# Two perceiver attention stages, walked four units at a time instead of two

## Chip, cores and metric

One core of one Trainium2 chip. The metric is the device time of one launch in microseconds (us): TensorE (PE) does the matrix products, VectorE (DVE), ScalarE (ACT) and GpSimd (POOL) the elementwise work, SyncE (SP) starts DMAs. Everything here is float32.

## The reference, cut to what matters

Four layers of attention and feed-forward run one after the other over `x` of 8 x 256 x 256. The change touches the attention of layers 1 and 2 alone, called perceiver 1 (`p1`) and perceiver 2 (`p2`). For each of 8 batches:

```python
# layer 1 (perceiver 1): 8 heads of 64, keys and values from context rows and latent rows
kv = jnp.concatenate([layer_norm(ctx), layer_norm(latents)], axis=1) @ Wkv
k, v = jnp.split(kv, 2, axis=-1)
q, k, v = map(to_heads, (latents @ Wq, k, v))
q = l2norm(q) * q_scale
k = l2norm(k) * k_scale
sim = jnp.where(full_mask, jnp.einsum('bhid,bhjd->bhij', q, k) * SCALE, max_neg)
out = jnp.einsum('bhij,bhjd->bhid', softmax(sim), v)
return layer_norm(out @ Wo)
# layer 2 (perceiver 2): the same shape without mask, l2norm and the last layer_norm
```

`x + out` then goes to the next layer, whose LayerNorm statistics are taken as the sums are written.

## The kernel before

Softmax work is cut into **units**: one head, 128 query rows, 512 keys. There are 8 batches x 8 heads x 2 halves of the rows, so 128 units per perceiver. Eight units make a **group** `g` (one batch, four heads), 16 groups in all. A unit goes through five steps:

- scores (`scores`, PE): one product with 64 contraction rows and 512 columns. Two units of a pair sit in the upper and the lower 64 rows of the array.
- maximum (`largest`, DVE): in p1 one custom operation that adds the mask, negates and takes the minimum (L1692); in p2 a reduction (L1696).
- exponential with its sum (ACT, L1567 in p1, L1570 in p2).
- reciprocal and scaling (DVE, L1671 and L1673).
- four 128x128 transposes (PE, L1486), emptied by ACT (L1581); after four units `values` (PE, L1512) multiplies by V.

Besides the units there are **pieces**. `make` produces what the next group needs: j = 0 and 1 two halves of K, j = 2 the queries, j = 3 and 4 two halves of V, each 4 matrix products (L1445, L1449). In p1 each of j = 0 to 2 is then normed: square on ACT (`sq`, L1542), sum per head on DVE (`ss`, L1632), reciprocal root on POOL (`rs`, L206 and L207), product on DVE (`nrm`, L1637), transposes on PE (L1460), and a copy on ACT (L1548). In p2 DVE copies the first three out at once (L1644, L1646). `out` is the product by Wo for a whole batch (L1429, every second group); in p1 it is followed by statistics (DVE), reciprocal root (POOL), norm (DVE, L1619), an affine step of four operations (POOL, L1715 and L1716) and the residual sum (DVE, L215 to L217), in p2 by the residual sum alone. `context` norms, transposes and stores the next context rows.

Each engine runs its own list in program order and waits on counters. The lists are made by hand: `agenda` maps a place in units (steps of 0.5) to pieces, and all engines walk i = 0, 2, 4, ... with two units each time. PE gives the scores of units i and i+1, then transposes units i-2 and i-1, and the values come two to four units later; so an exponential has a whole round of other work on PE in front of its transposes. PSUM: banks 0 and 1 hold scores, 2 and 3 transposes, 4 values, 5 to 7 pieces.

Of the kernel before, what the change touches and what calls it, by code (L numbers as in the profile page):

```python
# [6 lines left out]
ALU = mybir.AluOpType  # L7
# [1275 lines left out]
class Perceiver:  # L1283
# [5 lines left out]
    N = 128  # L1289

    def __init__(self, k, which, heir, affine_x, affine_z):
# [35 lines left out]
        vs = (0, 0.5)  # L1327
        if which == 1:
            kq, context, out = (0, 0.5, 1.5, 2.5, 3), (0.5, 2.5, 3), (0, 0.5, 1, 2.5, 6, 7)
            steps, order = ((0, (0, 0.5, 1.5, 3, 1.75)), (1, kq), (3, kq), (4, vs), (5, vs)), (1, 0, 2, 3, 4)  # L1330
        else:
            context, out = (0, 2.5, 3), (0, 0.5, 1)
            steps, order = ((0, vs), (1, vs), (3, vs), (4, vs), (5, vs)), range(5)
        self.agenda = {}
        for g in range(16):
            if g > 0 and g % 2 == 0:
                self.spread(8 * g + 6, out, "out", g // 2 - 1, 0)
            if g < 15:
                for j in order:
                    self.spread(8 * g + steps[j][0], steps[j][1], "make", g + 1, j)  # L1340
            if g == 0 or g % 2 == 1 and g < 13:
                self.spread(8 * g + 4, context, "context", 1 if g == 0 else g // 2 + 2, 0)
        self.early = [("context", 0, 0, s) for s in range(3)] + [("make", 0, j, s) for j, s in ((0, 0), (3, 0), (3, 1))]
        self.first = []
        for x in range(40):
            for j, (at, parts) in enumerate(steps):
                if x / 4 - at in parts and ("make", 0, j, parts.index(x / 4 - at)) not in self.early:
                    self.first.append(("make", 0, j, parts.index(x / 4 - at)))
        self.last = [("out", 7, 0, s) for s in range(len(out))]
        takes_m, takes_u, takes_n = [], [], []  # L1350
        for i in range(-1, 2 * self.N + 9):
            for kind, g, j, s in (self.early + self.first if i < 0 else self.pieces(i / 2) if i < 2 * self.N + 8 else self.last):
                key = (kind, g, j)
                if s == (1 if kind == "context" else 0):
                    takes_m.append(key)
                if which == 1 and kind == "make" and j < 3:
                    if s == 1:
                        takes_n.append(key)
                    if s == 3:
                        takes_u.append(key)  # L1360
        self.M = Turns((6, 7) if which == 1 else (5, 6, 7), takes_m)
        self.U, self.Z = Turns((5,), takes_u), Turns((0, 1, 2), takes_n)
        k.leave()

    def spread(self, at, parts, *what):
        for s, part in enumerate(parts):
            self.agenda.setdefault(at + part, []).append((*what, s))

    def pieces(self, at):
        return self.agenda.get(at, ())  # L1370
# [10 lines left out]
    def free_m(self, t, key):  # L1381
        was = self.M.before(key)
        if was is None:
            return
        kind, g, j = was
        if kind == "context":
            t.wait_ge(self.cxe, g + 1)
        elif kind == "out":
            t.wait_ge(self.opx if self.which == 2 else self.oy, g + 1)
        elif j >= 3:  # L1390
            t.wait_ge(self.val, 2 * g + j - 2)
        else:
            t.wait_ge(self.nrm if self.which == 1 else self.made, 3 * g + j + 1)

    def free_z(self, seat, key):

        was = self.Z.before(key)
        if was is None:
            return
        seat.wait_ge(self.zt, 3 * was[1] + was[2] + 1)  # L1400
# [10 lines left out]
    def pe_piece(self, t, kind, g, j, s):  # L1411
        k, key = self.k, (kind, g, j)
        if kind == "context":
            if s == 1:
                bk = k.bank(self.M.bank(key))
# [6 lines left out]
        elif kind == "out":  # L1422
            if s < 2:
                bk = k.bank(self.M.bank(key))
                if s == 0:
                    self.free_m(t, key)
                    t.wait_ge(self.oev, 2 * g + 2)
                for c in range(4):
                    ins = t.e.matmul(bk[:, s * 256:(s + 1) * 256], self.OT[:, c, s * 128:(s + 1) * 128], self.wo[:, c, :],  # L1429
                                     start=c == 0, stop=c == 3)  # L1430
                if s == 1:
                    ins.then_inc(self.opm.sem, 1)
        elif s == 0:
            b, hg = divmod(g, 2)
            at = slice(hg * 256, hg * 256 + 256)
            bk = k.bank(self.M.bank(key))
            self.free_m(t, key)
            t.wait_ge(*self.ready_w)
            half = (0, 1, 1, 0, 1)[j]
            x = self.rows_of(t, b, half)  # L1440
            w = (self.wk, self.wk, self.wq, self.wv, self.wv)[j]
            if j >= 3 or self.which == 1:
                for i in range(2):
                    for c in range(2):
                        ins = t.e.matmul(bk[:, i * 256:(i + 1) * 256], x[:, c, i * 128:(i + 1) * 128], w[:, c, at], start=c == 0, stop=c == 1)  # L1445
            else:
                for i in range(2):
                    for c in range(2):
                        ins = t.e.matmul(bk[:, i * 256:(i + 1) * 256], w[:, c, hg * 256 + i * 128:hg * 256 + (i + 1) * 128], x[:, c, :],  # L1449
                                         start=c == 0, stop=c == 1)  # L1450
            ins.then_inc(self.vmm.sem if j >= 3 else self.mm.sem, 1)
        elif s == 3:
            z, T, e = self.kn[self.Z.bank(key)], k.bank(5), 3 * g + j
            was = self.U.before(key)
            if was is not None:
                t.wait_ge(self.made, 3 * was[1] + was[2] + 1)
            t.wait_ge(self.nrm, e + 1)
            for c in range(2):
                for i in range(2):
                    ins = t.e.transpose(T[:, (2 * c + i) * 128:(2 * c + i + 1) * 128], z[:, i * 256 + c * 128:i * 256 + (c + 1) * 128], k.ident[:, :])  # L1460
            ins.then_inc(self.zt.sem, 1)

    def pe(self, t):
# [8 lines left out]
        for i in range(0, self.N + 4, 2):  # L1472
            if i < self.N:
                self.scores(t, i)
                self.scores(t, i + 1)
            for x in range(2):
                for at in (i + x, i + x + 0.5):
                    for p in self.pieces(at):
                        self.pe_piece(t, *p)
                u = i - 2 + x  # L1480
                if 0 <= u < self.N:
                    T = k.bank(2 + u % 2)
                    t.wait_ge(self.pt, u - 1)
                    t.wait_ge(self.scaled, u + 1)
                    for j in range(4):
                        ins = t.e.transpose(T[:, j * 128:(j + 1) * 128], self.P[u % 4][:, j * 128:(j + 1) * 128], k.ident[:, :])  # L1486
                    ins.then_inc(self.turned.sem, 1)
# [1195 lines left out]
```

## Time and profile before

| | |
|---|---|
| time, median of 3 runs | 1835.99 us (1834.31 to 1837.7) |
| profiled execution | 1833.89 us, of which the span 1832.1 us |
| busy share of the span | PE 86%, DVE 57%, ACT 49%, POOL 21% |
| chain that ended last | PE 69%, DVE 15%, ACT 6%, issue 5%, POOL 2% |

The share of an engine is the sum of its records over the whole span. The chain is followed back from the last instruction, at each step to what released it. p1's units run from about 519 to 908 us, p2's from about 1049 to 1405 us, about 40% of the span together.

### The profile page before, as it was taken

To read this page: it belongs to the slowest core of one execution; us is meant where nothing else is said; L and a number is where in the kernel's file an instruction comes from. 1 tells how busy PE (TensorE), PEld (TensorE's weight loads), DVE (VectorE), ACT (ScalarE), POOL (GpSimd) and SP (SyncE) were. 2 spreads that over 40 slices of the span, in tenths; PEclk is the share of its full clock that TensorE was granted. 3 is DMA by queue.
4 is the path that set the end of the run, shared out by engine and by line. 5 is a ranking of instruction groups with operands and counts; after the bars stand their busy time and mean duration, and the time that the engine had idled before them with its cause. 6 is when DMAs were issued, how large, how long until landed. Compare 5 with 4: busy or idle time off the path is not lost.

```text
span 1832.1 us, 27965 instructions
## 1 busy us (share of the span) xinstructions
PE 1579.8 (86%) x9902; PEld 1199.2 (65%) x9902; DVE 1050.6 (57%) x2956; ACT 906.7 (49%) x2034; POOL 380.5 (21%) x480
## 2 busy tenths in 40 slices
PE   7999958999489999999868799999998749995566
PEld 5677637999357676676536666666665548994444
DVE  7767752211546676766577665555555424325887
ACT  4888821332156666666449355555554102323366
POOL 1000014111232333323140100000001332323734
PEclk9999988999799999999978899999999979997889
DMA  9000027998300000000000200000000328993001
GB/s 339 6 1 1 2 92 305 323 330 290 118 7 7 7 7 7 7 1 1 1 1 1 81 12 7 6 7 6 1 1 12 138 81 297 355 348 112 1 12 35
DMA packets 61882, 154.08 MB, mean 84 GB/s; under 512 B 9232, under 2 KB 39696, under 8 KB 55248
## 3 DMA queue, kind: packets, MB, share of 16 engines
q1 hardware_dynamic: 54352, 135.73, 21.6%
q0 software_dynamic: 5280, 14.47, 2.1%
q10 hardware_dynamic: 2112, 2.10, 0.4%
q8 instruction: 80, 1.31, 0.3%
q14 instruction: 58, 0.48, 0.1%
HBM read 135.71 MB, written 24.75 MB: 88 GB/s over the span
## 4 chain that ended last, share of the span: by engine, by line
PE 69%; DVE 15%; ACT 6%; issue 5%; POOL 2%; DMA 1%; another core or an unknown queue 1%; POOLq 1%; SPq 0%; DVEq 0%; ACTq 0%
PE bank L1024 8%; PE bank L1445 8%; PE bank L974 7%; PE bank L1499 7%; PE bank L1512 6%; PE bank L1486 5%; PE bank L1449 5%; PE bank L1429 3%; PE bank L679 3%; PE bank L1851 2%; PE bank L695 2%; PE bank L710 1%; ACT p1f L1567 1%; PE bank L616 1%; POOL small L207 1%
## 5 line engine op out<-in xcount | busy, mean ns | idle before, releaser
L1696 DVE TENSOR_REDUCE small<-bank 128x1 f32<-128x512 f32 x128 | 82.4, 686 | 108.7 <-PE bank L1499 108.7
L1043 ACT ACTIVATE e2a<-bank,WB 128x128 f32<-128x128 f32 x156 | 44.6, 368 | 177.6 <-PE bank L1024 122.7
L1692 DVE CUSTOM_DVE_ANT_0 p1f<-bank,p1f 128x512 f32<-128x512 f32 x128 | 83.2, 687 | 81.3 <-PE bank L1499 81.3
L1570 ACT ACTIVATE p2f<-bank,small 128x512 f32<-128x512 f32 x128 | 86.9, 683 | 86.2 <-DVE small L1696 86.2
L751 ACT ACTIVATE l<-l,small 128x256 f32<-128x256 f32 x256 | 108.9, 502 | 32.6 <-DVE small L817 32.2
L1567 ACT ACTIVATE p1f<-p1f,small 128x512 f32<-128x512 f32 x128 | 91.2, 713 | 67.9 <-DVE small L1692 67.6
L400 POOL TENSOR_SCALAR rs<-mv 128x4 f32<-128x4 f32 x16 | 3.6, 228 | 566.7 <-DVEq L230 551.7
L817 DVE CUSTOM_DVE_ANT_0 l<-bank,small 128x256 f32<-128x256 f32 x256 | 90.8, 420 | 13.4 <-PE bank L695 12.5
L1445 PE MATMUL bank<-WA,HT 128*128 128x256 f32 x384 | 93.1, 386 | 5.0 <-DVE p1f L1637 5.0
L1581 ACT ACTIVATE p2f<-bank 128x512 f32<-128x512 f32 x128 | 75.2, 599 | 40.5 <-PE bank L1486 39.0
L1043 ACT ACTIVATE e0a<-bank,WB 128x128 f32<-128x128 f32 x128 | 36.6, 368 | 102.1 <-PE bank L1024 102.1
L207 POOL TENSOR_TENSOR small<-small,nhalf 128x8 f32<-128x8 f32 x48 | 80.5, 1678 | 4.0
L1581 ACT ACTIVATE p1f<-bank 128x512 f32<-128x512 f32 x128 | 74.2, 590 | 13.2 <-PE bank L1486 13.2
L1445 PEld LDWEIGHTS bank<-WA,HT 128*128 128x128 f32 x384 | 70.3, 193 | 14.6 <-DVE p1f L1637 5.6
L1024 PEld LDWEIGHTS bank<-e2a,WB 128*128 128x128 f32 x624 | 75.6, 192 | 5.8 <-issue 3.9
L1024 PE MATMUL bank<-e2a,WB 128*128 128x128 f32 x624 | 76.2, 274 | 3.1 <-DVE e2a L1192 3.1
L1486 PE MATMUL bank<-ident,p1f 128*128 128x128 f32 x512 | 75.0, 275 | 3.4 <-ACT p1f L1581 2.2
L1486 PEld LDWEIGHTS bank<-ident,p2f 128*128 128x128 f32 x512 | 61.0, 141 | 23.6 <-ACT p2f L1581 13.3
L1486 PEld LDWEIGHTS bank<-ident,p1f 128*128 128x128 f32 x512 | 59.9, 141 | 24.5 <-ACT p1f L1581 17.4
L1499 PE MATMUL bank<-p1f 64*128 64x512 f32 x256 | 73.5, 644 | 2.2 <-ACT p1f L1548 2.2
L1486 PE MATMUL bank<-ident,p2f 128*128 128x128 f32 x512 | 74.7, 275 | 0.0
L1499 PE MATMUL bank<-p2f 64*128 64x512 f32 x256 | 73.6, 641 | 1.1 <-ACT p2f L1570 1.1
(388 smaller groups left out, 3832.2 us busy)
## 6 DMA issues: line engine op xcount, KB each, us to landing
WB<-in_L2pack SPq DMA_DIRECT2D x39, 514.0 KB
WB<-in_L2pack SPq DMA_DIRECT2D x39, 512.0 KB
WB<-in_L0pack SPq DMA_DIRECT2D x16, 1028.0 KB
WB<-in_L0pack SPq DMA_DIRECT2D x16, 1024.0 KB
e0a<-in_L0pack SPq DMA_DIRECT2D x7, 1028.0 KB
e0a<-in_L0pack SPq DMA_DIRECT2D x7, 1024.0 KB
sorted_h<-in_blank SPq DMA_DIRECT2D x6, 1032.0 KB, 16.2
e2a<-sorted_h SPq DMA_DIRECT2D x39, 129.0 KB
```

The source lines that it names most:

```text
L207: g.e.tensor_tensor(dst, dst, self.nhalf[:, 0:n], ALU.pow).then_inc(flag.sem, 1)
L751: ins = a.e.activation(P[:, h * 256:(h + 1) * 256], P[:, h * 256:(h + 1) * 256], ACT.Exp, scale=-1.0, bias=self.mx[:, m + h:m + h + 1])
L817: ins = v.e.tensor_tensor_reduce(P[:, h * 256:(h + 1) * 256], k.bank(x)[:, h * 256:(h + 1) * 256], self.causal[:, h, :], -1.0, 3.0e38, ALU ...
L974: ins = t.e.matmul(y[:, 0:256], self.gb[i % 2][:, c, :], w[:, self.n1 + c * 256:self.n1 + (c + 1) * 256], start=c == 0, stop=c == nf - 1)
L1024: ins = t.e.matmul(bk[:, j * 128:(j + 1) * 128], w[:, c * ff + ft * 128:c * ff + ft * 128 + 128], self.xT[i % 2][:, c, :], start=c == 0, s ...
L1445: ins = t.e.matmul(bk[:, i * 256:(i + 1) * 256], x[:, c, i * 128:(i + 1) * 128], w[:, c, at], start=c == 0, stop=c == 1)
L1449: ins = t.e.matmul(bk[:, i * 256:(i + 1) * 256], w[:, c, hg * 256 + i * 128:hg * 256 + (i + 1) * 128], x[:, c, :], start=c == 0, stop=c == 1)
L1486: ins = t.e.transpose(T[:, j * 128:(j + 1) * 128], self.P[u % 4][:, j * 128:(j + 1) * 128], k.ident[:, :])
L1499: t.e.matmul(k.bank(i % 2), self.Q[g % 2][rows, c, a * 128:(a + 1) * 128], self.K[g % 2][rows, c, :], start=True, stop=True).then_inc(self ...
L1512: ins = t.e.matmul(k.bank(4)[64 * o:64 * o + 64, c * 256:c * 256 + 256], self.V[g % 2][:, j, h * 64:(h + 1) * 64], self.PT[n % 2][o][:, j, ...
L1567: ins = a.e.activation(P, P, ACT.Exp, scale=-1.0, bias=self.mx[:, m:m + 1], accum_out=self.sm[:, m:m + 1])
L1581: a.e.activation(self.PT[u // 4 % 2][o][:, :, h * 128:(h + 1) * 128], k.bank(2 + u % 2).rearrange("p (k n) -> p k n", k=4), ACT.Copy).then ...
```

## The change

The four steps of a walk (scores, maxima, exponentials, transposes) now take four units at a time, a **visit**; 32 visits per perceiver, `q` = 0 to 31. Group g has visit a = 2g and visit b = 2g+1. Inside a visit each engine has numbered parts, and the agenda is written with (engine, visit, part). Transposes of a visit's own units follow in the same visit, and `values` opens the next one. Scores and transposes of unit u share bank u mod 4, and banks 5 to 7 serve all pieces, p1's transposes of keys and queries included, which go back into the bank of their product. DVE takes the maxima of units 0 and 1 in part 0, of units 2 and 3 in part 1, and scales in parts 2 and 3; its pieces stand ahead of the unit work of their part. The sums and the number of operations are the same.

```diff
-        for i in range(0, self.N + 4, 2):
-            if i < self.N:
-                self.scores(t, i)
-                self.scores(t, i + 1)
-            for x in range(2):
-                for at in (i + x, i + x + 0.5):
-                    for p in self.pieces(at):
+        for q in range(self.QUADS + 1):
+            if q:
+                self.values(t, q - 1)
+            if q == self.QUADS:
+                break
+            for x in range(4):
+                self.scores(t, 4 * q + x)
+            for x in range(4):
+                if x % 2 == 0:
+                    for p in self.pieces("pe", q, x // 2):
                         self.pe_piece(t, *p)
...
+                self.turn_unit(t, 4 * q + x)
+            for p in self.pieces("pe", q, 2):
+                self.pe_piece(t, *p)
...
+                for j, at in ((0, (a, 0, a, 0)), (1, (a, 0, a, 0)), (2, (a, 1, a, 2)), (3, (b, 0, b, 0)), (4, (b, 0, b, 2))):
+                    if self.which == 1 and j == 3:
+                        put("pe", b, 0, "make", n, 1, "turn")
+                    put("pe", at[0], at[1], "make", n, j, "mm0")
+                    put("pe", at[2], at[3], "make", n, j, "mm1")
+                    if self.which == 1 and j == 2:
+                        put("pe", a, 2, "make", n, 0, "turn")
+                    if self.which == 1 and j == 4:
+                        put("pe", b, 1, "make", n, 2, "turn")
+                if self.which == 1:
+                    for j, sq, ss, rs, nrm, ev in ((0, (a, 1), (a, 3), (a, 2), (a, 4), (b, 0)), (1, (a, 2), (a, 4), (a, 3), (a, 5), (b, 1)),
+                                                   (2, (b, 0), (b, 1), (b, 0), (b, 3), (b, 3))):
+                        put("ac", *sq, "make", n, j, "sq")
+                        put("dv", *ss, "make", n, j, "ss")
+                        put("po", *rs, "make", n, j, "rs")
+                        put("dv", *nrm, "make", n, j, "nrm")
+                        put("ac", *ev, "make", n, j, "ev")
...
+                else:
+                    for j, ev in ((0, (a, 2)), (1, (a, 3)), (2, (b, 0))):
+                        put("dv", *ev, "make", n, j, "ev")
...
+                    put("dv", b + 1, 1, "out", o, 0, "st")
+                    put("po", b + 1, 0, "out", o, 0, "fac")
+                    put("dv", b + 1, 2, "out", o, 0, "nrm")
+                    put("po", b + 1, 1, "out", o, 0, "aff")
+                    put("dv", b + 2, 4, "out", o, 0, "add")
+                else:
+                    put("dv", b + 1, 1, "out", o, 0, "add")
...
+        for q in range(self.QUADS):
+            for pt in range(6):
+                for p in self.pieces("dv", q, pt):
                     self.dv_piece(v, *p)
+                if pt < 2:
+                    self.largest(v, 4 * q + 2 * pt)
+                    self.largest(v, 4 * q + 2 * pt + 1)
+                elif pt < 4:
+                    self.scale_unit(v, 4 * q + 2 * pt - 4)
+                    self.scale_unit(v, 4 * q + 2 * pt - 3)
```

ACT takes the four exponentials, with the pieces of part 1 in the middle, then empties the four transposes.

(In the new file, the scores are L1519, transposes L1527, values L1540, `make` L1479 and L1481, maxima L1735 and L1739, reciprocal L1719, scaling L1721, context transposes L1440, POOL's affine step L1758 and L1759.)

**PE in p2, four units.** Before, two pairs of scores (L1499) with `make` products and transposes (L1486) between, up to the values (L1512):

```order
L1499 MATMUL bank<-p2f 128x512 x2
L1449 MATMUL bank<-WB 128x256 x4
L1486 MATMUL bank<-ident,p2f 128x128 x4
L1449 MATMUL bank<-HT,WB 128x256 x4
L1486 MATMUL bank<-ident,p2f 128x128 x4
L1499 MATMUL bank<-p2f 128x512 x2
L1486 MATMUL bank<-ident,p2f 128x128 x4
L1449 MATMUL bank<-HT,WB 128x256 x4
L1486 MATMUL bank<-ident,p2f 128x128 x4
L1512 MATMUL bank<-p2f 64x256 x8
```

After, one visit b: behind the four scores stand the product j = 3 and the first half of j = 4, then all sixteen transposes of the visit, the second half of j = 4 and the context transposes (L1440):

```order
L1519 MATMUL bank<-p2f 128x512 x4
L1479 MATMUL bank<-WB 128x256 x4
L1479 MATMUL bank<-WB,HT 128x256 x2
L1527 MATMUL bank<-ident,p2f 128x128 x16
L1479 MATMUL bank<-WB,HT 128x256 x2
L1440 MATMUL bank<-ident,p2f 128x128 x4
L1540 MATMUL bank<-p2f 64x256 x8
```

The two islands of scores have become one, and the transposes now belong to the units whose scores stand just ahead.

**DVE in p2, where the residual sum of a finished batch stands.** Before, it followed the maxima and scalings of a pair:

```order
L1696 TENSOR_REDUCE small<-bank 128x1 x2
L1671 RECIPROCAL small<-small 128x1
L1673 TENSOR_SCALAR p2f<-p2f,small 128x512
L1671 RECIPROCAL small<-small 128x1
L1673 TENSOR_SCALAR p2f<-p2f,small 128x512
L215 TENSOR_TENSOR X<-bank,X 128x256
L200 BN_STATS st<-X 128x6
L201 BN_AGGR mv<-st 128x2
L217 TENSOR_TENSOR X<-bank,X 128x256
L200 BN_STATS st<-X 128x6
L201 BN_AGGR mv<-st 128x2
L1696 TENSOR_REDUCE small<-bank 128x1 x2
```

After:

```order
L1739 TENSOR_REDUCE small<-bank 128x1 x2
L215 TENSOR_TENSOR X<-bank,X 128x256
L200 BN_STATS st<-X 128x6
L201 BN_AGGR mv<-st 128x2
L217 TENSOR_TENSOR X<-bank,X 128x256
L200 BN_STATS st<-X 128x6
L201 BN_AGGR mv<-st 128x2
L1739 TENSOR_REDUCE small<-bank 128x1 x2
L1719 RECIPROCAL small<-small 128x1
L1721 TENSOR_SCALAR p2f<-p2f,small 128x512
```

The sum has moved between the second and the third maximum of a visit, ahead of the first scaling.

**POOL in p1, at the end of a batch.** Before, the reciprocal root of the output (rs) was followed by those of three `make` pieces (small), and the affine step came last:

```order
L207 TENSOR_TENSOR rs<-rs,nhalf 128x2
L206 TENSOR_SCALAR small<-small 128x8
L207 TENSOR_TENSOR small<-small,nhalf 128x8
L206 TENSOR_SCALAR small<-small 128x8
L207 TENSOR_TENSOR small<-small,nhalf 128x8
L206 TENSOR_SCALAR small<-small 128x8
L207 TENSOR_TENSOR small<-small,nhalf 128x8
L1715 TENSOR_TENSOR WB<-WB,rows 128x256
L1716 TENSOR_TENSOR WB<-WB,rows 128x256
L1715 TENSOR_TENSOR WB<-WB,rows 128x256
L1716 TENSOR_TENSOR WB<-WB,rows 128x256
```

After:

```order
L207 TENSOR_TENSOR rs<-rs,nhalf 128x2
L1758 TENSOR_TENSOR WB<-WB,rows 128x256
L1759 TENSOR_TENSOR WB<-WB,rows 128x256
L1758 TENSOR_TENSOR WB<-WB,rows 128x256
L1759 TENSOR_TENSOR WB<-WB,rows 128x256
L206 TENSOR_SCALAR small<-small 128x8
L207 TENSOR_TENSOR small<-small,nhalf 128x8
L206 TENSOR_SCALAR small<-small 128x8
L207 TENSOR_TENSOR small<-small,nhalf 128x8
L206 TENSOR_SCALAR small<-small 128x8
L207 TENSOR_TENSOR small<-small,nhalf 128x8
```

The four affine operations have moved ahead of the three reciprocal roots on which the next group's keys and queries wait.

## Rows read from the trace of the kernel before

**Rows 1.** Busy time by engine in stretches of p1 (two) and p2

```profile
core 0: us, PE busy (x) PEld busy (x) DVE busy (x) ACT busy (x) POOL busy (x), PEclk, DMA share, GB/s
518.70:534.00 15.30, 14.38 (x63) 9.82 (x64) 9.52 (x25) 8.65 (x18) 5.49 (x6) 0.89 0.01 1
534.00:907.60 373.60, 365.82 (x2134) 254.97 (x2134) 249.03 (x675) 235.46 (x517) 115.47 (x134) 1.00 0.02 5
1049.50:1405.00 355.50, 353.63 (x2021) 244.73 (x2020) 208.62 (x485) 194.27 (x445) 0.00 (x0) 1.00 0.02 5
```

**Rows 2.** Timeline of PE in p1: start us, us, engine, line, operation, count

```profile
601.48 0.60 PE L1486 MATMUL bank<-ident,p1f 128*128 128x128 f32 x4
602.01 1.95 PE L1512 MATMUL bank<-p1f 128*64 128x256 f32 x16
603.89 1.13 PE L1499 MATMUL bank<-p1f 64*128 64x512 f32 x4
604.95 1.99 PE L1445 MATMUL bank<-WA,WB 128*128 128x256 f32 x8
606.78 0.60 PE L1486 MATMUL bank<-ident,p1f 128*128 128x128 f32 x4
607.22 1.89 PE L1445 MATMUL bank<-WA,HT 128*128 128x256 f32 x8
608.95 0.60 PE L1460 MATMUL bank<-ident,p1f 128*128 128x128 f32 x4
```

**Rows 3.** Timeline of p2 near its end, scores to reciprocal

```profile
1393.95 1.13 PE L1499 MATMUL bank<-p2f 64*128 64x512 f32 x4
...
1395.11 1.29 DVE L1696 TENSOR_REDUCE small<-bank 128x1 f32<-128x512 f32 x2 [1.65 <-PE bank L1499]
1395.84 0.69 ACT L1570 ACTIVATE p2f<-bank,small 128x512 f32<-128x512 f32 x1 [1.17 <-DVE small L1696]
...
1396.65 0.16 DVE L1671 RECIPROCAL small<-small 128x1 f32<-128x1 f32 x1 [0.25 <-ACT p2f L1570]
```

**Rows 4.** Timeline of DVE in p1, scalings back to back

```profile
558.44 0.16 DVE L1671 RECIPROCAL small<-small 128x1 f32<-128x1 f32 x1
558.63 0.49 DVE L1673 TENSOR_SCALAR p1f<-p1f,small 128x512 f32<-128x512 f32 x1
559.03 0.16 DVE L1671 RECIPROCAL small<-small 128x1 f32<-128x1 f32 x1
```

**Rows 5.** Timeline near p1's end, POOL, scaling, its transposes

```profile
891.36 0.79 POOL L1716 TENSOR_TENSOR WB<-WB,rows 128x256 f32<-128x256 f32 x1
...
891.67 0.76 DVE L1673 TENSOR_SCALAR p1f<-p1f,small 128x512 f32<-128x512 f32 x1
...
892.55 0.42 PEld L1486 LDWEIGHTS bank<-ident,p1f 128*128 128x128 f32 x4 [0.45 <-issue]
```

**Rows 6.** Timeline of p1's drain, emptying and values

```profile
904.57 1.09 ACT L1581 ACTIVATE p1f<-bank 128x512 f32<-128x512 f32 x2 [0.26 <-PE bank L1486]
905.71 0.29 PEld L1512 LDWEIGHTS bank<-p1f 128*64 128x64 f32 x4 [0.93 <-ACT p1f L1581]
```

**Rows 7.** Timeline of a norm in p1, ss to nrm

```profile
510.21 0.69 DVE L1632 TENSOR_REDUCE small<-p1f 128x8 f32<-128x512 f32 x1 [4.21 <-ACT p1f L1542]
510.99 0.24 POOL L206 TENSOR_SCALAR small<-small 128x8 f32<-128x8 f32 x1 [5.71 <-DVE small L1632]
...
513.01 0.69 DVE L1637 TENSOR_TENSOR p1f<-bank,small 128x512 f32<-128x512 f32 x1 [2.12 <-POOL small L207]
```

**Rows 8.** Timeline of p1's last output, statistics to affine step

```profile
913.46 0.43 DVE L200 BATCH_NORM_STATS2 st<-bank 128x6 f32<-128x256 f32 x1 [9.40 <-PE bank L1429]
...
915.85 1.00 DVE L1619 TENSOR_SCALAR WB<-bank,mv,rs 128x256 f32<-128x256 f32 x2 [1.21 <-POOL rs L207]
916.92 0.72 POOL L1715 TENSOR_TENSOR WB<-WB,rows 128x256 f32<-128x256 f32 x1 [1.18 <-DVE WB L1619]
...
919.33 0.72 POOL L1716 TENSOR_TENSOR WB<-WB,rows 128x256 f32<-128x256 f32 x1
```

**Rows 9.** Timeline of p2's last residual sum, both halves

```profile
1409.53 0.42 DVE L215 TENSOR_TENSOR X<-bank,X 128x256 f32<-128x256 f32 x1 [8.73 <-PE bank L1429]
...
1410.55 0.39 DVE L217 TENSOR_TENSOR X<-bank,X 128x256 f32<-128x256 f32 x1
```

More of the change, by code:

```diff
@@ new lines, in __init__ @@
+        self.first = [("make", 0, j, p) for j, p in order]
+        self.last = [("out", 7, 0, p) for p in ("mm0", "mm1", "st", "fac", "nrm", "aff", "add")]
+        takes = [x[0:3] for x in self.early + self.first if x[3] in ("turn", "mm") and (x[0] == "context" or x[3] == "mm")]
+        for q in range(self.QUADS):
+            for pt in range(3):
+                takes += [x[0:3] for x in self.pieces("pe", q, pt) if x[3] == {"context": "turn", "make": "mm0", "out": "mm0"}[x[0]]]
+        self.M = Turns((5, 6, 7), takes + [("out", 7, 0)])
@@ L1334, in __init__, with plan @@
+        k.leave()
+    def plan(self):
         self.agenda = {}
+        put = self.put
         for g in range(16):
-            if g > 0 and g % 2 == 0:
[L1337 to L1340, printed above, removed]
-            if g == 0 or g % 2 == 1 and g < 13:
-                self.spread(8 * g + 4, context, "context", 1 if g == 0 else g // 2 + 2, 0)
@@ L1343, in __init__ @@
[L1343 to L1360, printed above, removed]
@@ L1372, in weights, with put, pieces @@
+            if g == 0 or g % 2 == 1 and g < 13:
+                c = 1 if g == 0 else g // 2 + 2
+                put("dv", b - 1, 5, "context", c, 0, "norm")
+                put("pe", b, 2, "context", c, 0, "turn")
+                put("ac", b + 1, 0, "context", c, 0, "ev")
+    def put(self, engine, q, pt, *what):
+        self.agenda.setdefault((engine, q, pt), []).append(what)
+    def pieces(self, engine, q, pt):
+        return self.agenda.get((engine, q, pt), ())
     def weights(self, W, ready):
@@ L1392, in free_m @@
         else:
[L1393 to L1400, printed above, removed]
+            t.wait_ge(self.made, 3 * g + j + 1)
     def rows_of(self, seat, b, j):
@@ L1428, in pe_piece @@
                 for c in range(4):
-                    ins = t.e.matmul(bk[:, s * 256:(s + 1) * 256], self.OT[:, c, s * 128:(s + 1) * 128], self.wo[:, c, :],
+                    ins = t.e.matmul(bk[:, i * 256:(i + 1) * 256], self.OT[:, c, i * 128:(i + 1) * 128], self.wo[:, c, :],
                                      start=c == 0, stop=c == 3)
-                if s == 1:
+                if i == 1:
                     ins.then_inc(self.opm.sem, 1)
[L1433 to L1456, printed above, removed]
+        elif s == "mm":
+            self.made_pe(t, key, bk, 0)
+            self.made_pe(t, key, bk, 1)
+        elif s in ("mm0", "mm1"):
+            self.made_pe(t, key, bk, int(s[2]))
+        elif s == "turn":
+            e = 3 * g + j
+            z = self.kn[e % 3]
             t.wait_ge(self.nrm, e + 1)
```

233 lines of the change are left out of this document (124 added, 109 removed).

## The prediction

> **What bounds the kernel now.** I read the two perceiver stretches first, then the order of PE inside them. PE is busy 365.82 of 373.60 us in p1 after its first 15 us and 353.63 of 355.50 us in p2, at full clock [rows 1]; no other engine is over two thirds. So before the change the program text of PE sets the pace, and only two things can change the time: what PE's own list costs, and whether the new order makes PE wait.
>
> PE's list, from the starts of its groups [rows 2]: the values take 1.88 us to the next start, a pair of scores 1.06, a `make` piece of four products 1.83 behind scores, four transposes 0.53 ahead of values and 0.44 ahead of a `make`, and a `make` in that place 1.73 (607.22 to 608.95). The same work costs 0.09 to 0.10 more on each side of a group that uses the array in halves (64 rows or 64 columns).
>
> **What the list gains.** Four scores together need two changes less per visit. The second pair no longer adds 0.09 to the transposes ahead and 0.10 to the `make` behind: 0.19. Inside, four products of 256 columns take 1.73 [rows 2], 0.43 each, so 512 columns 0.86 for two units side by side, against 1.06 for a pair alone: 0.20 more. I take 0.4 per visit, four scores 1.91 us; if only the neighbours gain, 0.19. 32 visits per perceiver: 12.8 us each (6.1 at the low end), 25.6 together. The waits PE had before are replaced too: 7.8 us in p1, 1.9 us in p2 [rows 1].
>
> **What a visit must now wait for.** Count from the first score, one visit at a time. Before, transposes came a round behind their exponentials; now the first transposes of a visit wait for scores, all four maxima, one exponential and one scaling of the same visit. The handovers: scores to maximum 1.16, maximum to exponential 0.73, exponential to reciprocal 0.81 [rows 3]; maxima follow each other in 0.60 (1.29 for two of 0.69) [rows 3]; reciprocal to scaling 0.19, and the next reciprocal 0.59 after the first [rows 4]; scaling 0.49 [rows 4], then 0.12 to PE (891.67 + 0.76 against 892.55) [rows 5]. An emptying of 0.6 is followed by values 0.05 later (905.66, 905.71) [rows 6].
>
> - p2, visit b. Maxima 1.16 to 3.56, scaling at 3.75, transposes possible at 4.36. Until then PE has scores 1.91, j = 3 1.83 and half of j = 4 0.86: 4.60. No wait for the first, but the scalings come every 0.59 and PE wants them every 0.44, so the fourth starts at 6.13 instead of 5.92. Loss 0.2, 15 visits: 3.2 us.
> - p2, visit a. PE has 5.47 us in front; DVE copies out j = 0 and 1 between. Some 0.1, 15 visits: 1.5 us.
> - p2, a visit a after a finished batch. The residual sum (1.02 for one half, so 2.04 [rows 9]) stands between the second and the third maximum. It runs from 2.36 to 4.40, maxima 3 and 4 to 5.60, the copy of j = 0 to 6.20, scaling 6.39, transposes 7.00 instead of 5.47. Loss 1.6 beyond the plain visit. Batches end seven times; the seventh falls into the last group. 6 visits: 9.7 us.
> - p1, visit b. One `ss` of 0.60 more ahead of maximum 3: scaling at 4.35, transposes at 4.96. PE has 1.91 + 0.49 (key transposes) + 1.73 + 0.86 = 4.99 in front. Then scalings lag as in p2, and the query's `nrm` and its transposes stand in the middle: the fourth transposes start at 7.33 instead of 6.75. Loss 0.58, 15 visits: 8.7 us.
> - p1, visit a, plain. `ss` of j = 0 about 4.8, `nrm` 2.80 later (510.21 to 513.01) [rows 7], its transposes at about 8.4; PE gets there at 8.95. No loss. `nrm` of j = 0 stands ahead of `ss` of j = 1 on DVE, but that chain ends before the next visit's first maximum.
> - p1, a visit a after a finished batch. Statistics start at 2.36; the norm 2.39 later at 4.75, the affine step 1.07 after that at 5.82; its four operations take 0.80 each (three in 919.33 - 916.92) [rows 8], until 9.03. Only then does POOL turn to the reciprocal root of j = 0, which was due about 7.7. 2.02 us (510.99 to 513.01) [rows 7] later, at 11.05, `nrm` starts, 0.75 more and PE may transpose at 11.80, where it was due at 8.95. Queued behind are values and the next scores, so all engines wait. Loss 2.85, 6 visits: 17.1 us. In five of them `nrm` of j = 1 and a context piece then end after the next first maximum was due, some 0.4: 2 us.
> - The last group of each perceiver has no `make`, thus no cover. Visit a with its output work: fourth transposes at 8.2, emptied and handed over 1.3 later (transposes 0.60 [rows 2], emptying 0.6 and the handovers [rows 6]), values at 9.5 where PE alone would need 3.87 (1.91 + 4 x 0.44 + 0.2); visit b likewise 7.45. Losses 5.6 and 3.6: 9.2 us in each perceiver.
>
> **The sum.** p1: -12.8 - 7.8 + 8.7 + 17.1 + 2 + 9.3 = +16.5. p2: -12.8 - 1.9 + 3.2 + 1.5 + 9.7 + 9.2 = +8.9. Together +25.4 on the profiled execution of 1833.89, so 1859.3; the median of the runs stands 2.1 us above that execution: **1861 us**. The start of each perceiver (up to the first score) has the same pieces in the same sequence, the loads are untouched (a context row's load waits for its transposes, due a whole group later), and bank turns find their bank free: each piece's bank was emptied at least a visit part earlier. I cost these at nothing. For the bank of the first half of j = 4 in p1 that cover is thin: ACT empties j = 1 by about 4.07 and PE takes the bank at 4.13; if it is late, visit b loses what it is late by, 0.1 us being 1.5 us in all.
>
> One price goes either way. A scaling beside a POOL operation of 0.79 took 0.76 instead of 0.49 [rows 5]; in the six visits with the affine step all four scalings now lie beside it. The fourth would start its transposes near 10 instead of 8.9, and PE then reaches the key's transposes near 11.3, still before 11.80, so I take nothing on PE's side; the affine step itself takes 0.07 longer per operation, 1.7 us over six visits, and not more than 0.5 per scaling, 12 us. The Trainium skill ("SBUF — State Buffer", SBUF: two separate sides) says that DVE and GpSimd hold a shared pair of ports exclusively and the loser waits for the whole instruction. By that rule POOL could lose as well as DVE, which speaks for the upper of these two ends; the trace shows DVE losing.
>
> **The rivals.**
> 1. *PE's list alone decides: faster.* Fewer changes between halves and whole array, waits hidden. Time 1836 - 25.6 - 9.7 = 1801. It decides if scores to first transposes takes under 4.6 us everywhere and the roots of j = 0 find POOL free. For it: plain visits nearly reach this. Against: 4.36 and 4.96 leave 0.2 at most, and the POOL chain of 11.8 is 2.85 too long. Chance 0.08. The Trainium skill ("TensorEngine Tiling (Array Packing)", Key Properties) says that changing the tiling mode drains the engine; by that rule this is the change's whole effect, and it names no wait against it.
> 2. *Half of the waits are hidden* (handovers shorter than in the drain rows, last visits partly overlapped): between 1811 and 1840, 1832 to 1840 being no change. Chance 0.12.
> 3. *The clock falls in the long waits.* The first 15.3 us of p1, with waits of some us, had a mean granted clock of 0.89 [rows 1]: 3.4 us at the lower level (1.2 GHz), 1.7 us of work lost. If each of the 13 visits with output work costs that, +22: 1883; at twice that 1905. Against it: waits of 1.6 to 2.9 us in visits of over 12 leave PE 80% busy. Chance 0.08.
> 4. *The walk above.* Chance 0.72, its own range 1840 to 1885: down if handovers are 0.1 shorter and the last groups lose less, up if four scores gain only 0.19 (+13.4) and POOL loses time to scalings (+12).
>
> **How the numbers follow.** The range 1838 to 1888 leaves out rival 1, most of rival 2, half of rival 3 and the walk's edges, about 0.2. What a measurement of this kernel can tell from no change is 0.2%, 3.7 us. Faster: rival 1 and the lower part of 2, 0.13. Same: 0.06. Slower: 0.81.
>
> **What would show it.** In the changed kernel: L1519 x4 followed 1.91 us later by the next start (2.12 would say the inner gain is none). In plain visits the first L1527 5.5 us (a) and 4.6 or 5.0 us (b) after the first score. In p1's visits with L1758, the transposes of j = 0 start 11.8 us after the scores, with PE waiting on DVE's product and POOL's roots. p1 from first score to last values some 405 us instead of 389, p2 364 instead of 355.5. The prediction is wrong if these visits are no longer than plain ones, if the scores to transposes chain is over 5 us in all b visits (then each 0.1 costs 3 us), or if the clock row falls below 0.97 in these stretches.

## The result

The changed kernel takes 1857.24 us (median of 4 runs, 1854.07 to 1861.3), the kernel before 1835.15 (4 runs, 1828.65 to 1837.7) beside it: ratio 1.0113, 95% interval 1.0093 to 1.0132. It is slower by 22 us; forecast were 1861 and 25.

The profiled execution of the changed kernel took 1854.07 us. Three lines of its page:

```profile
span 1851.4 us, 27656 instructions
...
PE 1570.1 (85%) x9894; PEld 1194.8 (65%) x9902; DVE 1030.1 (56%) x2956; ACT 908.4 (49%) x2034; POOL 383.1 (21%) x480
...
PE 69%; DVE 16%; issue 4%; ACT 4%; POOL 3%; another core or an unknown queue 2%; DMA 1%; POOLq 1%; SPq 0%; DVEq 0%; ACTq 0%
```

The last line is the chain of work that ended last. Its shares are nearly those of before (DVE 16% against 15%), so they do not show where the time went. The stretches do (busy time by engine; they answer to [rows 1]):

```profile
core 0: us, PE busy (x) PEld busy (x) DVE busy (x) ACT busy (x) POOL busy (x), PEclk, DMA share, GB/s
534.00:920.40 386.40, 363.50 (x2104) 250.67 (x2102) 236.69 (x665) 235.26 (x508) 117.80 (x133) 0.99 0.02 5
1057.50:1421.80 364.30, 348.88 (x2021) 245.93 (x2020) 197.41 (x485) 192.88 (x445) 0.00 (x0) 1.00 0.02 5
```

PE has less busy time than before in p2 (348.9 against 353.6) and idles 15.4 us instead of 1.9; in p1 it idles 22.9 instead of 7.8. From the first score to the end of the last values, p1 went from 390.3 to 405.0 us (+14.7, forecast +16.5) and p2 from 355.6 to 364.2 (+8.6, forecast +8.9). The granted clock is 0.99 and 1.00. The two profiled executions differ by 20.2 in all, their spans by 19.3: p1 and p2 make +23.3, the way to p1's first score -3.3 (515.4 instead of 518.7), the way from p1 to p2 -3.3 (137.1 instead of 140.5) and what follows p2 +2.6. The code between p1 and p2 and behind p2 was not changed but for the starts of the two classes; what the start of p1 has to do with the first of these numbers stands further down.

**A plain visit.** PE's timeline of one visit a in p1 without output work (start us, us, engine, line, operation, count), the same columns as [rows 2]:

```profile
613.37 1.99 PE L1519 MATMUL bank<-p1f 64*128 64x512 f32 x8
615.29 1.99 PE L1479 MATMUL bank<-WA,WB 128*128 128x256 f32 x8
617.12 1.89 PE L1479 MATMUL bank<-WA,HT 128*128 128x256 f32 x8
618.85 1.04 PE L1527 MATMUL bank<-ident,p1f 128*128 128x128 f32 x8
619.72 1.03 PE L1479 MATMUL bank<-WA,HT 128*128 128x256 f32 x4
620.59 1.04 PE L1527 MATMUL bank<-ident,p1f 128*128 128x128 f32 x8
```

Four scores to the next start: 615.29 - 613.37 = 1.92 (1.91 forecast). The first transposes follow 5.48 after the scores (5.5), one group comes directly behind the other, and the visit is 11.36 long, as the walk has it. So PE's list has the length that the walk gave it. By how much it is shorter than before is measured further down.

**A visit with output work in p1.** The timeline of a visit a behind a finished batch, all engines, without the rows between that do not matter here; a bracket is the idle time before and what ended it. It answers to [rows 5, 7, 8]:

```profile
587.25 1.99 PE L1519 MATMUL bank<-p1f 64*128 64x512 f32 x8
...
592.04 0.99 DVE L1661 TENSOR_SCALAR WB<-bank,mv,rs 128x256 f32<-128x256 f32 x2
593.11 0.72 POOL L1758 TENSOR_TENSOR WB<-WB,rows 128x256 f32<-128x256 f32 x1 [1.18 <-DVE WB L1661]
593.14 0.98 DVE L1721 TENSOR_SCALAR p1f<-p1f,small 128x512 f32<-128x512 f32 x1
594.17 0.66 PE L1527 MATMUL bank<-ident,p1f 128*128 128x128 f32 x4 [1.29 <-DVE p1f L1721]
594.22 0.76 DVE L1721 TENSOR_SCALAR p1f<-p1f,small 128x512 f32<-128x512 f32 x1
594.91 0.67 DVE L1674 TENSOR_REDUCE small<-p1f 128x8 f32<-128x512 f32 x1
595.65 0.73 POOL L1759 TENSOR_TENSOR WB<-WB,rows 128x256 f32<-128x256 f32 x1
595.68 0.97 DVE L1721 TENSOR_SCALAR p1f<-p1f,small 128x512 f32<-128x512 f32 x1
596.46 0.30 POOL L206 TENSOR_SCALAR small<-small 128x8 f32<-128x8 f32 x1
596.84 1.94 POOL L207 TENSOR_TENSOR small<-small,nhalf 128x8 f32<-128x8 f32 x1
598.81 0.69 DVE L1679 TENSOR_TENSOR p1f<-bank,small 128x512 f32<-128x512 f32 x1 [1.56 <-POOL small L207]
599.56 0.66 PE L1464 MATMUL bank<-ident,p1f 128*128 128x128 f32 x4 [0.73 <-DVE p1f L1679]
```

The affine step starts 5.86 after the scores (5.82 forecast) and POOL turns to the root at 9.21 (9.03). The root then takes 2.35 instead of 2.02, `nrm` starts at 11.56 (11.05) and the transposes of j = 0 at 12.31 (11.80). The visit is 14.76 long, 3.40 more than a plain one, where 2.85 was forecast. The fourth scaling (596.76, beside the root) took 0.48.

**The same in p2**, with the residual sum between second and third maximum (timeline of DVE and PE; the scores began at 1123.07); it answers to [rows 3, 9]:

```profile
1125.44 0.42 DVE L215 TENSOR_TENSOR X<-bank,X 128x256 f32<-128x256 f32 x1
...
1127.43 1.25 DVE L1739 TENSOR_REDUCE small<-bank 128x1 f32<-128x512 f32 x2
...
1129.39 0.49 DVE L1721 TENSOR_SCALAR p2f<-p2f,small 128x512 f32<-128x512 f32 x1
```

The sum begins 2.37 after the scores (2.36), the first scaling 6.32 (6.39), and PE takes it at 1129.94, 6.87 after (7.00). The visit is 12.57 long, a plain one 11.00.

**The last group.** The clock was not full everywhere. PE's timeline of the last visits a, in p1 and in p2, and behind them the stretches of p1 ahead of its last group and inside it, with the columns of the stretches above:

```profile
896.09 1.99 PE L1519 MATMUL bank<-p1f 64*128 64x512 f32 x8
903.00 3.71 PE L1527 MATMUL bank<-ident,p1f 128*128 128x128 f32 x16 [4.92 <-DVE p1f L1721]
907.45 3.62 PE L1540 MATMUL bank<-p1f 128*64 128x256 f32 x16 [0.73 <-issue]
911.00 1.99 PE L1519 MATMUL bank<-p1f 64*128 64x512 f32 x8
...
1406.49 3.28 PE L1527 MATMUL bank<-ident,p2f 128*128 128x128 f32 x16 [4.28 <-DVE p2f L1721]
```

```profile
534.00:896.09 362.09, 347.89 (x2024) 241.78 (x2022) 221.98 (x621) 223.92 (x483) 113.78 (x127) 1.00 0.02 5
900.60:910.90 10.30, 7.16 (x32) 4.78 (x32) 4.80 (x12) 3.64 (x8) 3.25 (x5) 0.50 0.00 0
```

Inside PE's wait of 4.92 us the granted clock fell to 0.50, which is 1.2 GHz, for about 10 us. The values of that visit took 3.62 us instead of 1.95, so the next scores came 3.55 behind them instead of 1.88. In p2 the same visit has a wait of 4.28, the clock was at 0.50 from about 1405.8 to 1409.2, and its transposes took 3.28 us, where the next visit's took 2.44.

### The profile page after: what moved, and what is told of

Read it like the earlier page. It is cut to its first block, busy times and chain, and to the rows that moved or that the text cites. A ratio compares the mean times of both kernels' runs of the same rounds, so it can differ in the third digit from the quotient of the medians.

```text
span 1851.4 us, 27656 instructions
## 1 busy us (share of the span) xinstructions
PE 1570.1 (85%) x9894; PEld 1194.8 (65%) x9902; DVE 1030.1 (56%) x2956; ACT 908.4 (49%) x2034; POOL 383.1 (21%) x480
## 4 chain that ended last, share of the span: by engine, by line
PE 69%; DVE 16%; issue 4%; ACT 4%; POOL 3%; another core or an unknown queue 2%; DMA 1%; POOLq 1%; SPq 0%; DVEq 0%; ACTq 0%
PE bank L1479 9%; PE bank L1024 8%; PE bank L974 7%; PE bank L1540 7%; PE bank L1527 6%; PE bank L1519 6%; PE bank L1481 4%; PE bank L1449 3%; PE bank L679 3%; PE bank L695 2%; PE bank L1895 2%; PE bank L710 2%; PE bank L1464 1%; PE bank L616 1%
## 5 line engine op out<-in xcount | busy, mean ns | idle before, releaser
L1739 DVE TENSOR_REDUCE small<-bank 128x1 f32<-128x512 f32 x128 | 79.9, 682 | 136.4 <-PE bank L1519 136.4
L1735 DVE CUSTOM_DVE_ANT_0 p1f<-bank,p1f 128x512 f32<-128x512 f32 x128 | 82.5, 687 | 100.1 <-PE bank L1519 100.1
L1479 PE MATMUL bank<-WA,HT 128*128 128x256 f32 x384 | 96.7, 382 | 0.8 <-ACT p1f L1576 0.8
L1527 PE MATMUL bank<-ident,p1f 128*128 128x128 f32 x512 | 76.6, 285 | 17.1 <-DVE p1f L1721 16.7
L1622 ACT ACTIVATE p2f<-bank 128x512 f32<-128x512 f32 x128 | 69.6, 597 | 32.7 <-PE bank L1527 31.3
L207 POOL TENSOR_TENSOR small<-small,nhalf 128x8 f32<-128x8 f32 x48 | 81.9, 1706 | 4.0
L1527 PE MATMUL bank<-ident,p2f 128*128 128x128 f32 x512 | 70.8, 283 | 13.9 <-DVE p2f L1721 13.9
L1527 PEld LDWEIGHTS bank<-ident,p1f 128*128 128x128 f32 x512 | 56.8, 143 | 39.2 <-DVE p1f L1721 36.9
L1527 PEld LDWEIGHTS bank<-ident,p2f 128*128 128x128 f32 x512 | 58.4, 143 | 28.5 <-DVE p2f L1721 22.2
L1479 PEld LDWEIGHTS bank<-WA,HT 128*128 128x128 f32 x384 | 68.4, 191 | 11.1 <-ACT p1f L1576 3.0
L1721 DVE TENSOR_SCALAR p1f<-p1f,small 128x512 f32<-128x512 f32 x128 | 71.4, 558 | 4.5
L974 PE MATMUL bank<-WB,e2a 128*128 128x256 f32 x312 | 73.6, 379 | 0.0
```

The costliest lines, as they stand in the source:

```text
L974: ins = t.e.matmul(y[:, 0:256], self.gb[i % 2][:, c, :], w[:, self.n1 + c * 256:self.n1 + (c + 1) * 256], start=c == 0, stop=c == nf - 1)
L1622: a.e.activation(self.PT[u // 4 % 2][o][:, :, h * 128:(h + 1) * 128], self.k.bank(u % 4).rearrange("p (k n) -> p k n", k=4), ACT.Copy).the ...
L1735: v.e.tensor_tensor_reduce(self.P[m], k.bank(m), self.mb[b % 2], -1.0, 3.0e38, ALU.add, ALU.min, self.mx[:, m:m + 1]).then_inc(self.maxed. ...
```

## The experiments

Kernels that were timed together share a chip and its runs of the kernel before. Chips differ by 1%, so ratios and visits are compared, not times. A visit's length is from its first score to the next visit's first score.

**1. Each perceiver by itself.** Both forms of the class stand in the kernel, one perceiver uses the new, the other the old (the rest of the diff is the second copy of the class):

```diff
# p1_only
-        p1 = Perceiver(...)
-        p2 = Perceiver(...)
+        p1 = PerceiverFour(...)
+        p2 = PerceiverTwo(...)
# p2_only: the other way round
```

> Perceiver 1 walks four units per visit, perceiver 2 two units as before. Theory (each perceiver pays for its own waits): p1 stays some 15 us longer than before, p2 355 us as before, time about 1851. Rival (the loss sits in what lies between the stages, or in a lower clock that both share): p1_only and p2_only do not add up to the 22 us of the whole change.

> Perceiver 2 walks four units per visit, perceiver 1 two units as before. Theory: p2 364 us instead of 355.5, time about 1844, that is +9. Rival (PE's list alone decides where no norm and no POOL work is in the way): p2 343 us, time 1823.

Measured, beside 1815.62 us before: p1 alone 1826.96, ratio 1.0072 (1.0053 to 1.0091); p2 alone 1826.66, 1.0059 (1.0038 to 1.0081). Inside, p1 alone shows 405.0 us for p1 and 355.6 for p2, p2 alone 388.8 and 366.5. Each half is slower by itself, and 0.72 + 0.59 = 1.31% is, within the intervals, the 1.13% of the whole. That the loss lies between the stages, or that one half gains, is out.

**2. The affine step one visit later** (`aff_late`), which takes it from between the output's norm and the root of j = 0:

```diff
-                    put("po", b + 1, 1, "out", o, 0, "aff")
+                    put("po", b + 2, 0, "out", o, 0, "aff")
```

> The changed kernel with one edit: POOL's affine step of a finished batch in p1 stands in the next visit b, ahead of the root of j = 2, instead of ahead of the root of j = 0. Theory (the transposes of j = 0 wait for POOL, and scalings beside the affine step lose time): visits with output work fall from 14.8 to about 12.8 us, six of them, and the visits b behind them lose 0.25 less; 13 to 14 us in all, time about 1843. Rival (DVE's statistics and norm between the maxima are the whole wait): visits stay above 14.3, time above 1853.

Measured: 1827.07, ratio 1.0067 (1.0048 to 1.0085), on the chip of experiment 1. The visit with output work (timeline, its scores at 587.12):

```profile
593.01 0.49 DVE L1721 TENSOR_SCALAR p1f<-p1f,small 128x512 f32<-128x512 f32 x1
593.56 1.25 PE L1527 MATMUL bank<-ident,p1f 128*128 128x128 f32 x8 [0.80 <-DVE p1f L1721]
...
596.86 0.69 DVE L1679 TENSOR_TENSOR p1f<-bank,small 128x512 f32<-128x512 f32 x1 [0.97 <-POOL small L207]
597.60 0.66 PE L1464 MATMUL bank<-ident,p1f 128*128 128x128 f32 x4
```

The scaling is back at 0.49, `nrm` starts 9.74 after the scores instead of 11.56, and the visit is 12.94 long instead of 14.76: as expected. But the visit b behind it rose from 11.35 to 11.76, where 0.25 less was expected. About 8 us were gained instead of 13 to 14. The theory of POOL's row of work stands, since the visit lost 1.82; something else in visit b was not seen. Experiment 4 takes that up.

**3. The output's other pieces moved too** (`out_moved`): statistics ahead of the maxima, norm between them, the residual sum of p2 ahead of them:

```diff
# on top of aff_late
-                    put("dv", b + 1, 1, "out", o, 0, "st")
+                    put("dv", b + 1, 0, "out", o, 0, "st")
-                    put("dv", b + 1, 2, "out", o, 0, "nrm")
+                    put("dv", b + 1, 1, "out", o, 0, "nrm")
# p2
-                    put("dv", b + 1, 1, "out", o, 0, "add")
+                    put("dv", b + 1, 0, "out", o, 0, "add")
```

> The changed kernel with aff_late's edit, p1's output statistics ahead of the first maximum and its norm ahead of the third, and p2's residual sum ahead of the first maximum, where DVE is idle. Theory: visits a after a finished batch are as long as plain ones (11.4 in p1, 11.0 in p2): -20 and -9, -4 in the last groups, -1 behind; time about 1821, 0.8% faster than before the change. Rival (the norm or sum makes the first maximum late, and each tenth of it goes through to PE): visits of 12 us or more, time about 1832.

Measured: 1806.22, ratio 0.9952 (0.9937 to 0.9967): faster than before, by 0.5% where 0.8% was expected. In p2 the visits a behind a finished batch are now 11.00, the 1.57 of the residual sum is gone. In p1 such a visit is 11.75, 0.39 longer than a plain one, where none was expected; that rest was not looked into. The visit b behind it still has 11.76; its start (timeline, POOL and DVE beside the scores):

```profile
643.97 1.99 PE L1519 MATMUL bank<-p1f 64*128 64x512 f32 x8
644.09 0.73 POOL L1758 TENSOR_TENSOR WB<-WB,rows 128x256 f32<-128x256 f32 x1
644.16 0.69 DVE L1679 TENSOR_TENSOR p1f<-bank,small 128x512 f32<-128x512 f32 x1 [2.11 <-POOL small L207]
644.77 1.13 DVE L1641 TENSOR_SCALAR p1f<-p1f,cmv,crs 128x256 f32<-128x256 f32 x2
645.82 0.68 DVE L1735 CUSTOM_DVE_ANT_0 p1f<-bank,p1f 128x512 f32<-128x512 f32 x1
```

The first maximum comes 1.85 after the scores, not 1.16: `nrm` of j = 1 waited for POOL's root into this visit, and the context's norm (L1641, 1.13) stands behind it and lies beside the affine step.

**4. The context's norm ahead of that wait** (`ctx_early`):

```diff
# on top of out_moved
-                put("dv", b - 1, 5, "context", c, 0, "norm")
+                put("dv", b - 1, 4, "context", c, 0, "norm")
```

> out_moved with one edit: the norm of the next context rows stands one part earlier on DVE, ahead of p1's last nrm, in a wait of DVE on POOL. Theory (in out_moved the first maximum of the five visits b behind a context piece starts at 1.85 instead of 1.16 us, since nrm, the context norm and POOL's affine step end late): these visits fall from 11.8 to about 11.1 us, 3 us in all, 0.9935 of before. Rival (POOL's affine step ahead of the root of j = 2 is what makes them long): they stay at 11.7.

Measured on another chip, beside 1834.46 before: 1824.74, ratio 0.9941 (0.9921 to 0.996). The visit b behind output work fell from 11.76 to 11.25, its transposes start 5.01, 5.53, 6.89 and 7.48 after the scores. About 11.1 was expected. The ratio, 0.11 points lower than in experiment 3, lies within both intervals; the 0.5 us in each of five such visits is read from the trace, the total can't show it.

**5. Values behind the next scores** (`values_behind`), on the changed kernel and with its output work unmoved. The values of a visit wait for emptied transposes; here the next visit's four scores stand between:

```diff
         for q in range(self.QUADS + 1):
-            if q:
-                self.values(t, q - 1)
             if q == self.QUADS:
+                self.values(t, q - 1)
                 break
             for x in range(4):
                 self.scores(t, 4 * q + x)
+            if q:
+                self.values(t, q - 1)
```

> The changed kernel with one edit: PE gives the four scores of a visit first and the values of the visit before behind them, so the chain from scores to transposes has 1.9 us more of PE's work over it, and PE's list changes between halves and whole array as often as before. Theory (the cost of the change is the uncovered chain inside a visit): p1 visits a after a finished batch 12.9 instead of 14.8 us, p2's 11.0 instead of 12.6, visits b without their 0.2 to 0.6, the last groups 1.9 less per visit; 35 to 41 us off, about 0.99 of the time before the change. Rival (the length of the POOL chain and of DVE's list decides, whatever stands on PE): under 15 us off, time above 1.003 of before.

Measured: 1812.8, ratio 0.9892 (0.9865 to 0.9919), as expected. PE's timeline at a visit's start:

```profile
582.58 1.99 PE L1520 MATMUL bank<-p1f 64*128 64x512 f32 x8
584.50 1.95 PE L1541 MATMUL bank<-p1f 128*64 128x256 f32 x16
586.38 1.99 PE L1479 MATMUL bank<-WA,WB 128*128 128x256 f32 x8
```

The 1.88 of values now lie in front of the transposes and cover that much of the chain over ACT and DVE: in p2 all visits a but the last are 11.00 although the residual sum has not moved, p1's with output work 12.90 instead of 14.76. Had the waits not been the cause, turning two groups of PE round would have gained nothing.

**6. All three together** (`best`).

> out_moved, values_behind and ctx_early together. Theory: all visits but those of the last groups are as long as PE's own list; against out_moved 8.7 us less in p1's visits b, 3.5 in p2's, 4 behind batches, 7 in the last groups: about 0.98 of before. Rival (with values behind the scores ACT waits for them before the first exponential in each visit a, and the fourth scores wait for the last emptying): 0.99 or more.

Measured: 1797.53, ratio 0.9798 (0.9772 to 0.9823), the fastest of that chip. Between the first visit and the last group every visit a of p1 is 11.36 and of p2 11.00.

**7. The same with its scores in two pairs again** (`split_scores`), to price PE's list by itself, and the best version once more on that chip (`best_again`, unchanged):

```diff
-            for x in range(4):
+            for x in range(2):
                 self.scores(t, 4 * q + x)
             if q:
                 self.values(t, q - 1)
+            for x in range(2, 4):
+                self.scores(t, 4 * q + x)
```

> The kernel best with one edit: PE gives two scores of a visit ahead of the values of the visit before and two behind them, so its list changes once more per visit between tilings, with the same products. Theory (each change costs some 0.2 us on PE, also where no full array lies between): every visit 0.2 us longer, 12.8 us in all, about 0.987 of before. Rival (a change costs only where full-array work stands beside it, so halves by rows and halves by columns pass into each other free, or the cost hides in idle time): visits as long as in best, 0.980 of before.

> The kernel best once more, on the chip of split_scores, as what that run is to be held against: 0.980 of before within 0.3%.

Measured, beside 1814.4 before: the pairs 1796.39, ratio 0.99 (0.9882 to 0.9919); the best version 1777.57, 0.9801 (0.9783 to 0.9819). PE's timeline with pairs:

```profile
568.89 1.13 PE L1522 MATMUL bank<-p1f 64*128 64x512 f32 x4
569.95 1.95 PE L1543 MATMUL bank<-p1f 128*64 128x256 f32 x16
571.83 1.13 PE L1522 MATMUL bank<-p1f 64*128 64x512 f32 x4
572.89 0.66 PE L1464 MATMUL bank<-ident,p1f 128*128 128x128 f32 x4
```

Pair, values, pair take 4.00 to the next start (572.89 - 568.89); four scores and values take 3.79 in the best version (566.62 to 570.41). Each visit is 0.20 us longer, 11.56 instead of 11.36, 12.8 us over 64 visits. That is the price expected. The other 6 of the 18.8 us between the two do not belong to it. They lie in the last groups, 3.8 us in p1 and 3.5 in p2 beyond that price, less 1.4 that p1's first visit was shorter. In the last visit of p1 the first transposes come 6.06 after the first score instead of 4.35, and nothing covers it; in that of p2 it is 6.04 instead of 4.29. The larger part is the clock: over the last groups it was 0.85 and 0.86 with the pairs and 1.00 in the best version. The last values of p1: ```profile
885.78 3.68 PE L1543 MATMUL bank<-p1f 128*64 128x256 f32 x16 [0.69 <-ACT p1f L1625]
```

In the best version they took 1.95. The stretches of the best version, first score to last values, against 390.3 and 355.6 before:

```profile
510.70:877.90 367.20, 363.43 (x2200) 267.33 (x2200) 245.13 (x700) 242.20 (x534) 122.41 (x139) 0.99 0.02 5
1016.50:1362.60 346.10, 342.86 (x2021) 245.50 (x2020) 198.18 (x485) 190.73 (x445) 0.00 (x0) 1.00 0.02 5
```

PE idles 3.8 and 3.2 us. Both stretches are 23.1 and 9.5 us shorter than before.

## Why the prediction was right

The direction and the mechanism were right. So was the time, 1857 against 1861, but in p1 by luck: two errors of 8 and 10 us cancelled. By its steps:

- **PE's list, 0.4 per visit.** Nearly. Four scores take 1.92. Carried on to the next score, the walk's own terms give 11.36 and 10.61 for p1's visits a and b without output or context work and 11.04 and 9.41 for p2's (for a visit a of p1: 8.95 + 0.53 + 1.88); measured are 11.36, 10.65, 11.00 and 9.40. Against before, the gain is a little smaller: in the middle of p2, where PE had no idle time before, a batch of four visits is 44.3 us in the best version and was 45.6, which is 0.33 per visit. Experiment 7 measures one half alone: with the neighbours the same, one island of scores less is 0.20 per visit.
- **Visits b, 0.58 in p1 and 0.2 in p2.** Right: the fourth transposes start at 7.34 (7.33) and 6.07 (6.13).
- **The residual sum in p2, 1.6.** Right: 1.57, and experiment 3 removes it by moving the sum alone.
- **The affine step ahead of the root in p1, 2.85.** Right in place, too small: 3.40. The term took neither side's slowing on the path. The third scaling took 0.97, beside the last affine operation, and the root 2.35 instead of 2.02, beside the fourth; the affine step itself took 0.15 longer. That is the open price of the prediction, 3.3 us over six visits. Experiment 2, with the affine step gone from there, has scalings of 0.49 and gives 1.82 per visit back. The rule on exclusive ports (the Trainium skill, "SBUF — State Buffer", SBUF: two separate sides) lets either side lose, and the trace agrees in that: DVE 0.49 to 0.98, POOL's root 2.02 to 2.35. That the loser waits for a whole instruction is not shown: beside the fourth scaling of 0.48 the root's long operation lost 0.27. The prediction named POOL's side and put it in the range, not in the sum.
- **The visit behind it, 0.4.** 0.26.
- **The last groups, 9.2 each** (9.3 in the sum of p1). Visits b were right (7.47 and 7.41 against 7.45), visits a too short: the values start at 11.36 in p1 and 10.31 in p2 where both had 9.5. In p2 that is the lower clock: the transposes start 6.27 after the scores and take 0.84 longer than at the full one. In p1 the four scalings lie beside the affine step (0.98, then 0.76), and the clock is lower too; with the values of 3.62 the whole visit is 14.90 where the walk has 11.38, so the term was 3.5 too small.
- **The sum of p1: right by luck.** The prediction's sum gives 388.9 + 16.5 = 405.4 us for p1, measured are 405.0. But the lengths of p1's visits in the walk add up to 396.7 only. (This is an estimate. It takes 0.44 us for a context's transposes and 3.45 for an output product, the differences between visits b of the best version.) So the visits of the walk were 8.3 short: 3.3 for the roots, 3.5 for the last visit a, and 1.4 because p1's first four scores ran at the lower clock (3.42 us instead of 1.99).
- **The waits of before, 7.8 in p1: too small.** The walk's 396.7 is 6.4 more than the 390.3 that p1 took before, where the sum has 16.5. So the gains, -12.8 - 7.8, left out 10 us, and that is what made up for the 8.3. The 7.8 is PE's idle time from 534.00 to 907.60. Outside that stretch p1 had a first `make` piece at the lower clock (3.25 us instead of 1.99), 0.9 us idle and 1.4 us up to the end of the last values. Inside it, part of the last values ran at the lower clock (3.29 instead of 1.95), and a batch in the middle was 49.4 us, 1.2 more than the 46.7 of the best version and four times 0.4, while the records show 0.5 of it as idle. These make up most of the 10; the rest is not split.
- **Both together.** In p2 both ways of adding agree: 364.4 forecast, 364.2 measured. Held against the measured stretches before, the walk's lengths would have forecast about 15 us more (6.4 + 8.8) and not 25; measured are 23.3.
- **By batches.** From score to score, a batch in the middle of p1 (four visits) went from 26.07 + 23.34 us to 25.48 + 26.11, in p2 from 24.33 + 21.25 to 23.85 + 22.42: +2.2 and +0.7. Six of each make 17 of the 23.3 us; the first and the last groups give the other 6.
- **The start of each perceiver, put at nothing.** Not quite. Ahead of p1's first score the pieces come in the same sequence, but they have a bank more:

```profile
505.31 0.69 DVE L1637 TENSOR_TENSOR p1f<-bank,small 128x512 f32<-128x512 f32 x1 [2.12 <-POOL small L207]
506.06 3.49 PE L1445 MATMUL bank<-WA,HT 128*128 128x256 f32 x8 [4.31 <-DVE p1f L1637]
```

```profile
500.54 2.26 PE L1479 MATMUL bank<-WA,HT 128*128 128x256 f32 x8
```

Before (first fence), the product of j = 1 took the bank of j = 0 and waited for its norm. After, it starts 3.8 us ahead of that norm (504.31), and the root of j = 0 runs beside it. From DVE's last copy of the turned input rows (L318) to the first score the start took 13.8 us instead of 16.1. The clock has a part in that which these runs do not separate: the same new start took 13.8 to 16.2 us in the other kernels, the old one 16.5 in `p2_only`.

The rivals. That PE's list alone decides is out for this change, but its mechanism is real: once the waits are covered the kernel is 2.0% faster, where the forecast's price of the list and the waits of before gave 1.9% (1801 of 1836). The parts fit less well than the sum: p1 gained 23.1 to 24.8 us where 20.6 were forecast, p2 9.5 where it was 14.7. Which of the two effects decides is a matter of order, not of the number of units. Half-hidden waits are out: the handovers agree within 0.1. The falling clock as the rival had it, in each visit with output work, is out: the stretch up to the last group has 1.00. In the last groups the clock did fall, at a price of about 3 us in both together (an estimate: 1.7 for the values in p1, 0.8 for the transposes in p2, some 0.5 for p1's transposes). The Trainium skill's rule that a change of tiling mode drains the engine ("TensorEngine Tiling (Array Packing)", Key Properties) agrees with the 0.20 us per visit of experiment 7; as the change's whole effect, which rival 1 took it for, it is not borne out.

What was not seen before experiment 2: that moving work off POOL's row leaves `nrm` of j = 1 waiting across the visit's border, with the context's norm queued behind it and the next maxima behind that. The expectation counted only what the affine step had delayed, not what it would lie beside next. Experiment 4 confirms this by its first transposes at 5.01 instead of 5.68.

## What to carry to other kernels

Batching groups of like products saves engine changes, but it also takes away the distance between a producer and its consumer: count the new chain from the first product over every engine to where the list comes back to it, and count it in the visits with extra work apart, since those decided here. If the chain is too long, put independent work of the batch before in front (here the values, 1.88 us) and move side work ahead of the chain's first link; the same batching then turned from 1.1% slower to 2.0% faster. An operation that is moved off one queue's critical place must be followed to its new neighbours. And when a walk gives the length of every visit after, add these up and hold the total against the measured stretch before: a sum of gains and losses against PE's idle time missed 10 us here.

## What was not expected of the hardware

- A DVE scaling of 512 columns takes 0.49 us alone and 0.76 to 0.98 beside POOL's products; POOL loses too (a product 0.72 to 0.79). Beside a root the scaling kept 0.48 to 0.50, and the root's long operation took 1.72 to 1.94 instead of 1.67. DVE's reductions and its product out of a bank kept their 0.67 to 0.69.
- Between halves by rows (scores) and halves by columns (values) a second island of scores costs the same 0.20 us as between whole-array work: pair, values, pair 4.00 against 3.79, two pairs apart 2.12 against 1.92.
- PE's waits in the visits with output work, 2.4 us of idle time in 26 us, left the granted clock at 1.00. Inside the waits of 4.92 and 4.28 us in the last groups it fell to 0.50.
